# Layer 0 of a compressed interaction network: pairs of fields packed into full tiles, and a remainder stacked three times in one

## The chip, the cores and the metric

One core of a Trainium2 chip runs the whole program in one launch. The metric is the device time in microseconds. Engines are named PE (TensorE, matmul), DVE (VectorE), ACT (ScalarE), POOL (GpSimd) and SP (SyncE, which only issues DMAs here). The core has 16 DMA engines.

## The reference

2048 samples have 39 fields each; every field is an embedding row of 16 numbers, gathered from its own table. Three layers follow, with x0 the gathered fields and xk the first half of the layer before:

```
z = einsum('bhd,bkd,hks->bsd', x0, xk, W) + b     # 128 outputs s
z = relu(z); xk = z[:, :64]; direct.append(z[:, 64:])   # the last layer keeps all
logit = sum over d of concatenate(direct)
h = concatenate(logit, dense_ctx); three dense layers 272 -> 512 -> 256 -> 1
```

In layer 0 xk is x0 itself, so the product of fields f and g appears twice, and the kernel adds the two weights: 39 x 40 / 2 = 780 pairs of fields.

## The kernel before, in words

The samples go in 64 chunks of 32 samples, which with the 16 numbers of a row are 512 columns. POOL gathers the rows of a chunk by ten indirect DMAs, SP stores them turned into a DRAM tensor `x0_rows` of 58 rows (fields, and the first ones again) by 32768 columns, and SP and ACT load them back spread over partitions: `xa` (the 39 fields, three times below each other, 117 rows) and `xb` (the same fields shifted by 0, 1, 2 and then by 3 more for each of 7 tiles) for layer 0, `xh` (each field on 64 partitions, 20 tiles) for layers 1 and 2. A load of rows is 2 KB per row.

A layer is a sum over tiles: DVE multiplies a tile of `xb` or `xh` by the shared operand (`xa_ps`, a copy of `xa` in PSUM, or `x`, the relu output), and PE multiplies the product by the tile's weights into `z`. Three kinds of group share the cost of precision. WHOLE: the product and weights stay fp32, and a tile takes two instructions on PE. BY_DVE and BY_POOL: ACT rounds the product to fp32r (`high`, L877), DVE (L564) or POOL (L537) forms the remainder (`low`), and PE makes three fp32r passes: high by w_high, high by w_low, low by w_high. A half tile of layers 1 and 2 holds 64 products twice, so that its lower half can take the remainder (`half_passes`, two passes).

`GROUPS` lists, by stage (layer), the groups as (kind, first tile, number of tiles); all engines walk this list in its order, written out by hand. A step of the chunk loop is layer 1 of chunk c, layer 0 of chunk c + 1, layer 2 of chunk c. `load_pairs` (L415) on SP loads `xa` and `xb` once the products of layer 0 of the chunk before are made and the rows are stored; it stands between the stores and the load of `xh`, and before the store of features, which waits for sums that DVE makes right after layer 0. ACT's `copy_xa` (L863) is queued after the fifth rounding of layer 1 and waits for all pair loads; DVE's `layer0` (L623) waits for them and for the copy. SP, ACT and DVE each do their queue in order.

Before, layer 0 has 7 tiles: six of 3 shifts (117 rows) and one of 2 shifts (78 rows), in the groups WHOLE (tile 6), BY_DVE (0, 1), BY_POOL (2, 3), WHOLE (4, 5).

Of the kernel before, what the change touches and what calls it, by code (L numbers as in the profile page):

```python
# [28 lines left out]
CN = CB * D  # L29
# [9 lines left out]
T0 = -(-SHIFTS // JT)  # L39
LAST0 = (SHIFTS - JT * (T0 - 1)) * F  # L40
# [10 lines left out]
    0: [(WHOLE, 6, 1), (BY_DVE, 0, 2), (BY_POOL, 2, 2), (WHOLE, 4, 2)],  # L51
# [12 lines left out]
LAST_OUT_AFTER, XA_AFTER, FIRST_OUT_AFTER = 5, 4, 5  # L64
T1, T2 = 512, 256
# [6 lines left out]
STAGED = {0: 0, 1: T0, 2: T0 + TK}  # L72
TURNED = T0 + 2 * TK
ALL_TILES = TURNED + T0
# [20 lines left out]
class Group:  # L95


    def __init__(self, stage, chunk, g, counts, users):
# [7 lines left out]
        self.rows = 128 if stage else (LAST0 if first == T0 - 1 else JT * F)  # L106
# [19 lines left out]
def in_order_of_use(groups):  # L126

    behind = None
    for g in groups:
        late = g.split and not g.half  # L130
        if behind and (late or g.half or g.ends_layer):
# [56 lines left out]
def tower(nc, table, ids, row_base, ctx_t, staged, wt1, wt1c, wt2, cols, out):  # L188
# [6 lines left out]
    with ExitStack() as stack:  # L195
# [27 lines left out]
        xa = sb("xa", [JT * F, CN])  # L223
        xb = sb("xb", [JT * F, T0, CN])
# [34 lines left out]
        def split_places(weights, products):  # L259
# [8 lines left out]
                    "ctx": [w[0:CTX, CTX_AT:CTX_AT + MB], w[0:CTX, CTX_AT + MB:CTX_AT + 2 * MB]],  # L268
# [9 lines left out]
        assert ctx_end + MB // S <= len(SPLIT_TILE)  # L278
# [30 lines left out]
        x0_loaded = sem("x0_loaded")  # L309
        xa_copied = sem("xa_copied")  # L310
# [72 lines left out]
        N_GROUPS = len(firsts)  # L383
        W_READY = sum(g.split + g.half for g in firsts)
# [11 lines left out]
        def _(sp):  # L396
# [35 lines left out]
            def chunk(c):  # L432
# [7 lines left out]
                if not c.known or c.n >= 1:  # L440

                    wait_made(sp, 0, c - 1)
                load_pairs(c)
# [3 lines left out]
                elif c.n == 1:  # L447

                    sp.wait_ge(w_ready, W_READY)
                    sp.wait_ge(w_rounded, N_GROUPS)  # L450
# [15 lines left out]
            for i, (at, n) in enumerate([(0, T0), (TURNED, T0), (T0, TK), (T0 + TK, TK)]):  # L466
# [89 lines left out]
        def _(dve):  # L556
            def low_parts(g, c):
# [4 lines left out]
                part = slice(H, 128) if g.half else slice(0, g.rows)  # L562
                into = (high if g.half else low)[part, g.split_slot, 0:n, :]
# [5 lines left out]
            def products(stage, c, spread, shared, second=None):  # L569
# [3 lines left out]
                for g in groups(stage, c):  # L573
# [17 lines left out]
                    t = slice(g.tiles[0], g.tiles[0] + n)  # L591
                    dve.tensor_tensor(  # L592
# [452 lines left out]
```

## Time and profile before

| | |
|---|---|
| median of 3 runs | 2424.73 us (2424.66 to 2425.77) |
| profiled execution, its own time | 2426.18 us |
| its span, first to last instruction | 2424.2 us |
| PE busy | 2343.5 us, 97% |
| DVE busy | 2253.4 us, 93% |
| POOL busy | 2004.7 us, 83% |
| ACT busy | 1306.0 us, 54% |
| DMA queue q1 (SP) | 304354 packets, 310.69 MB, 52.9% of 16 engines |
| DMA queue q10 (ACT) | 78864 packets, 159.39 MB, 21.5% |
| mean granted clock of TensorE | 0.994 |

Busy time is the time in which an engine had an instruction under way. The share of the DMA is over the 16 DMA engines together; where transfers of one engine overlap it can read a little over 1. Matmuls are pipelined, so the pace of PE is the distance of their starts, not their length.

### The profile page before, as it was taken

Reading aid. Unit: us, or ns where it says so; the run is one execution under the profiler, and the core shown is the slowest. Engines: PE = TensorE matmul, PEld = TensorE weight load, DVE = VectorE, ACT = ScalarE, POOL = GpSimd, SP = SyncE. Lnnn points to the kernel's source line nnn. Section 1 sums busy time; section 2 is a strip of 40 time slices with the busy share of each in tenths; the row PEclk is TensorE's granted clock in tenths of the full one; section 3 lists DMA queues with packets and bytes.
Section 4 is the critical chain, followed back from the end, with each engine's and each line's share of the span. In section 5 each row is a group of like instructions: output and inputs, shape, how many; then the busy total and the mean of one; then the engine's idle time right before and its main releaser. Section 6 shows DMA issues by size and latency. Waiting matters only on the chain.

```text
span 2424.2 us, 32379 instructions
## 1 busy us (share of the span) xinstructions
PE 2343.5 (97%) x7936; PEld 1497.1 (62%) x7936; DVE 2253.4 (93%) x2241; ACT 1306.0 (54%) x1534; POOL 2004.7 (83%) x1284
## 2 busy tenths in 40 slices
PE   1699999999999999999999999999999999999999
PEld 0466666666666666666666666666666666666655
DVE  2699999999999999999999999999999999999973
ACT  2355555555555555555555555555555555555542
POOL 3689888988888898888889888888988888898630
PEclk9899999999999999999999999999999999999999
DMA  7878778877877887787788778778877877887710
GB/s 180 175 197 231 188 200 219 216 183 210 233 191 196 219 212 185 212 234 187 200 219 214 184 211 232 187 200 221 208 190 209 233 182 205 221 209 188 204 56 1
DMA packets 403715, 475.43 MB, mean 196 GB/s; under 512 B 171409, under 2 KB 180625, under 8 KB 403425
## 3 DMA queue, kind: packets, MB, share of 16 engines
q1 hardware_dynamic: 304354, 310.69, 52.9%
q10 hardware_dynamic: 78864, 159.39, 21.5%
q0 software_dynamic: 20480, 5.15, 1.8%
q8 instruction: 8, 0.13, 0.0%
q14 instruction: 9, 0.07, 0.0%
HBM read 465.41 MB, written 9.71 MB: 196 GB/s over the span
## 4 chain that ended last, share of the span: by engine, by line
PE 94%; POOL 2%; DMA 2%; issue 1%; SPq 0%; ACT 0%; DVE 0%; ACTq 0%; POOLq 0%
PE z L709 91%; POOL rows L507 1%; DMA xb<-x_rows 1%; POOL low L537 1%; DMA x_rows<-rows 1%; DMA rows<-table,index 0%; SPq L411 0%; PE x L804 0%; PE z L823 0%; PE prod_dve L804 0%; PE z L825 0%; PE z L782 0%; PE z L828 0%; PE x L805 0%; PE x L806 0%
## 5 line engine op out<-in xcount | busy, mean ns | idle before, releaser
L537 POOL TENSOR_TENSOR low<-prod_pool,high 128x1024 fp32r<-128x1024 f32 (+1 forms) x576 | 1379.9, 2396 | 220.8 <-ACT high L877 214.1
L709 PE MATMUL z<-prod_whole,w_whole 128*128 128x512 f32 (+2 forms) x2432 | 1129.4, 593 | 41.7 <-DVE prod_whole L592 41.7
L709 PE MATMUL z<-high,w_high 128*128 128x512 f32 (+1 forms) x1792 | 863.9, 482 | 31.2 <-ACT high L877 16.2
L877 ACT ACTIVATE high<-prod_pool 128x1024 fp32r<-128x1024 f32 (+1 forms) x576 | 610.9, 1061 | 405.8 <-DVE prod_pool L592 236.3
L709 PEld LDWEIGHTS z<-prod_whole,w_whole 128*128 128x128 f32 (+2 forms) x2432 | 460.9, 190 | 426.1 <-issue 364.1
L507 POOL DMA_INDIRECT rows<-table,index x640 | 613.5, 959 | 115.2 <-issue 99.7
L709 PE MATMUL z<-high,w_low 128*128 128x512 f32 (+1 forms) x1792 | 708.3, 395 | 0.0
L592 DVE TENSOR_TENSOR prod_pool<-xh,x 128x1024 f32<-128x1024 f32 x512 | 622.6, 1216 | 38.8 <-ACT x L855 33.6
L592 DVE TENSOR_TENSOR prod_whole<-xh,x 128x1024 f32<-128x1024 f32 (+1 forms) x576 | 615.7, 1096 | 7.6 <-PE z L709 1.6
L877 ACT ACTIVATE high<-prod_dve 128x1024 fp32r<-128x1024 f32 (+2 forms) x384 | 339.0, 883 | 497.0 <-DVE prod_dve L592 323.4
L709 PE MATMUL z<-low,w_high 128*128 128x512 f32 (+1 forms) x1664 | 553.5, 426 | 4.2 <-POOL low L537 4.2
L709 PEld LDWEIGHTS z<-high,w_high 128*128 128x128 f32 (+1 forms) x1792 | 339.5, 189 | 189.0 <-issue 112.2
L709 PEld LDWEIGHTS z<-high,w_low 128*128 128x128 f32 (+1 forms) x1792 | 339.9, 190 | 153.1 <-issue 91.2
L709 PEld LDWEIGHTS z<-low,w_high 128*128 128x128 f32 (+1 forms) x1664 | 313.8, 189 | 128.5 <-issue 60.3
L592 DVE TENSOR_TENSOR prod_dve<-xh,x 128x1024 f32<-128x1024 f32 (+1 forms) x320 | 323.8, 1012 | 15.3 <-DMA xh<-x_rows 10.9
L564 DVE TENSOR_TENSOR low<-prod_dve,high 128x1024 fp32r<-128x1024 f32 (+1 forms) x256 | 313.3, 1224 | 17.4 <-ACT high L877 13.1
L855 ACT ACTIVATE x<-z,cols_sb 64x512 f32<-64x512 f32 x256 | 166.6, 651 | 106.8 <-PE z L709 101.9
L592 DVE TENSOR_TENSOR prod_whole<-xb,xa_ps 78x512 f32<-78x512 f32 (+1 forms) x128 | 120.7, 943 | 23.4 <-ACT xa_ps L868 23.4
L564 DVE TENSOR_TENSOR high<-prod_dve,high 64x512 fp32r<-64x512 f32 x128 | 89.0, 695 | 9.8 <-ACT high L877 5.9
L860 ACT ACTIVATE direct<-z,cols_sb 64x512 f32<-64x512 f32 x128 | 87.7, 685 | 3.3
L592 DVE TENSOR_TENSOR prod_dve<-xb,xa_ps 117x1024 f32<-117x1024 f32 x64 | 78.0, 1219 | 0.0
L592 DVE TENSOR_TENSOR prod_pool<-xb,xa_ps 117x1024 f32<-117x1024 f32 x64 | 77.4, 1209 | 0.0
(59 smaller groups left out, 404.6 us busy)
## 6 DMA issues: line engine op xcount, KB each, us to landing
xh<-x_rows SPq DMA_DIRECT2D x63, 2560.0 KB, 17.8
xh<-x_rows ACTq DMA_DIRECT2D x63, 2432.0 KB, 19.2
xb<-x_rows SPq DMA_DIRECT2D x128, 546.0 KB
xb<-x_rows SPq DMA_DIRECT2D x64, 468.0 KB
xa<-x_rows SPq DMA_DIRECT2D x192, 78.0 KB
rows<-table,index POOLq DMA_INDIRECT x640, 5.4
xh<-x_rows SPq DMA_DIRECT2D x65, 128.0 KB, 20.5
x_rows<-rows SPq DMA_DIRECT2D x256, 20.0 KB, 1.6
```

Source lines behind the costliest of these rows:

```text
L507: pool.indirect_dma_start(rows_sb[p][0:n, j * D:(j + 1) * D], None, table, bass.IndirectOffsetOnAxis(ap=index[p][0:n, j:j + 1], axis=0),). ...
L537: pool.tensor_tensor(low[0:g.rows, g.split_slot, 0:n, :], prod_pool[0:g.rows, g.slot, 0:n, :], high[0:g.rows, g.split_slot, 0:n, :].bitcas ...
L564: dve.tensor_tensor(into, prod_dve_v[part, 0:n, :], high[part, g.split_slot, 0:n, :].bitcast(f32), ALU.subtract,).then_inc(low_by_dve, 1)
L592: dve.tensor_tensor(into[0:g.rows, 0:n, :], spread[0:g.rows, t, :], shared[0:g.rows, :].unsqueeze(1).broadcast_to([g.rows, n, CN]), ALU.mu ...
L709: return pe.matmul(z[stage][:, :], weights[0:g.rows, table[stage, g.tiles[i]], :], src[0:g.rows, i, :], start=g.begins_layer and first, st ...
L855: act.activation(xk[stage][half, :], z[stage][feed, :], ACT.Relu, bias=bias[stage][feed, :]).then_inc(relu_done[stage], 1)
L860: act.activation(direct[c.p][leave, :], z[stage][leave, :], ACT.Relu, bias=bias[stage][leave, :]).then_inc(relu_done[stage], 1)
L877: act.activation(high[0:g.rows, g.split_slot, 0:n, :], src[0:g.rows, 0:n, :], ACT.Copy).then_inc(high_ready, 1)
```

## The change

Layer 0 gets six tiles of 128 rows: the three shifts of 39 fields, and below them 11 more pairs (fields 0 to 10 with a field that lies 18 + tile further), loaded by two more DMAs of 11 rows. The last shift of the old tile 6 is gone; of its pairs, and of those not placed, 34 are left. They stand in a seventh tile, out of 40 rows that are loaded; pairs already placed have zero weights. The 40 rows stand at partitions 0 to 39 (their product is `high`, weighted by w_high), 64 to 103 (there DVE overwrites `high` with the remainder `low`, weighted by w_high), and in two halves of 20 at 40 to 59 and 104 to 123, both weighted by w_low (DVE overwrites 64 to 103 only, so these keep `high`). One pass on PE takes all three products. `xa_rest` is the first operand of that tile; it and the tile of `xb` are cleared once at the start by DVE. The 40 rows in their three places are loaded by 12 DMAs of 20 rows, each with the source pattern of 2 runs of 10 rows. The groups are now WHOLE (0, 1), BY_DVE (6, the rest), BY_POOL (2, 3), WHOLE (4, 5). The weights of the rest come from two staged tiles (one with the rows for w_high, one for w_low), joined by two DVE operations at the start.

```diff
-T0 = -(-SHIFTS // JT)
-LAST0 = (SHIFTS - JT * (T0 - 1)) * F
+T0 = SHIFTS // JT + 1
+REST = T0 - 1
+MORE = 128 - JT * F
+MORE_AT = JT * REST
+LEFT, LEFT_AT, LEFT_RUN, LEFT_STEP = 40, 10, 10, 19
+REST_LOW = 64
+FOR_HIGH_W = [(0, LEFT, 0), (0, LEFT, REST_LOW)]
+FOR_LOW_W = [(0, LEFT // 2, LEFT), (LEFT // 2, LEFT, REST_LOW + LEFT)]
...
-    0: [(WHOLE, 6, 1), (BY_DVE, 0, 2), (BY_POOL, 2, 2), (WHOLE, 4, 2)],
+    0: [(WHOLE, 0, 2), (BY_DVE, REST, 1), (BY_POOL, 2, 2), (WHOLE, 4, 2)],
...
+X0_LOADS = 2 * JT + 2 + 12
...
-        xa = sb("xa", [JT * F, CN])
-        xb = sb("xb", [JT * F, T0, CN])
+        xa = sb("xa", [128, CN])
+        xa_rest = sb("xa_rest", [128, CN])
+        xb = sb("xb", [128, T0, CN])
...
-                    "ctx": [w[0:CTX, CTX_AT:CTX_AT + MB], w[0:CTX, CTX_AT + MB:CTX_AT + 2 * MB]],
+                    "ctx": [w[0:CTX, CTX_AT:CTX_AT + MB], x[0:CTX, 4 + n1, :]],
...
             def load_pairs(c):
                 of = rows_of(c)
+                step = of.ap[0][0]
                 for jj in range(JT):
-                    n = (SHIFTS - jj + JT - 1) // JT
                     at = slice(jj * F, (jj + 1) * F)
                     sp.dma_start(xa[at, :], of[0:F, :]).then_inc(x0_loaded, 16)
-                    step = of.ap[0][0]
                     shifted = bass.AP(tensor=of.tensor, offset=of.offset + jj * step,
-                                      ap=[[step, F], [JT * step, n], [1, CN]])
-                    sp.dma_start(xb[at, 0:n, :], shifted).then_inc(x0_loaded, 16)
+                                      ap=[[step, F], [JT * step, REST], [1, CN]])
+                    sp.dma_start(xb[at, 0:REST, :], shifted).then_inc(x0_loaded, 16)
+                sp.dma_start(xa[JT * F:128, :], of[0:MORE, :]).then_inc(x0_loaded, 16)
+                shifted = bass.AP(tensor=of.tensor, offset=of.offset + MORE_AT * step,
+                                  ap=[[step, MORE], [step, REST], [1, CN]])
+                sp.dma_start(xb[JT * F:128, 0:REST, :], shifted).then_inc(x0_loaded, 16)
+                for first, end, to in FOR_HIGH_W + FOR_LOW_W:
+
+                    halves = range(2 * first // LEFT, 2 * end // LEFT)
+                    for s in halves:
+                        at = slice(to + (s - halves[0]) * LEFT // 2, to + (s - halves[0] + 1) * LEFT // 2)
+                        for rows, field in ((xa_rest, LEFT_AT + s), (xb[:, REST, :], LEFT_AT + LEFT_STEP)):
+                            runs = bass.AP(tensor=of.tensor, offset=of.offset + field * step,
+                                           ap=[[LEFT_STEP * step, 2], [step, LEFT_RUN], [1, CN]])
+                            sp.dma_start(rows[at, :], runs).then_inc(x0_loaded, 16)
...
-                part = slice(H, 128) if g.half else slice(0, g.rows)
-                into = (high if g.half else low)[part, g.split_slot, 0:n, :]
+                part = slice(H, 128) if g.half else slice(REST_LOW, REST_LOW + LEFT) if g.rest else slice(0, g.rows)
+                into = (high if g.stacked else low)[part, g.split_slot, 0:n, :]
...
+            dve.memset(xa_rest[:, :], 0.0).then_inc(rest_cleared, 1)
+            dve.memset(xb[:, REST, :], 0.0).then_inc(rest_cleared, 1)
...
+                def rest_pass(g):
+
+                    wait_count(pe, low_by_dve, c, g, g.of_kind + 1, BY_DVE)
+                    mm(g, w_high, SPLIT_TILE, high[:, g.split_slot, :, :], 0, True, True
+                       ).then_inc(products_used, 1)
...
-                act.wait_ge(x0_loaded, (c.n + 1) * 2 * JT * 16)
+                act.wait_ge(x0_loaded, (c.n + 1) * X0_LOADS * 16)
                 if not (c.known and c.n == 0):
                     wait_made(act, 0, c - 1)
-                act.activation(xa_ps[0:JT * F, :], xa[:, :], ACT.Copy).then_inc(xa_copied, 1)
+                act.activation(xa_ps[:, :], xa[:, :], ACT.Copy).then_inc(xa_copied, 1)
```

## Rows read from the trace of the kernel before

**Rows 1.** The page, part 1: busy us, share of the span, instructions.

```profile
PE 2343.5 (97%) x7936; PEld 1497.1 (62%) x7936; DVE 2253.4 (93%) x2241; ACT 1306.0 (54%) x1534; POOL 2004.7 (83%) x1284
```

**Rows 2.** Waits, whole span: engine, line, releaser, sum, times, longest.

```profile
PE z L709 <- DVE prod_whole L592: 41.7, 1, 41.7
ACT xa_ps L868 <- DMA xb<-x_rows: 37.0, 2, 22.9
DVE prod_pool L592 <- ACT x L855: 33.6, 64, 5.6
DVE prod_whole L592 <- ACT xa_ps L868: 23.4, 1, 23.4
```

**Rows 3.** Timeline of PE in layer 0: start, us, instruction, count.

```profile
1233.90 0.39 PE L709 MATMUL z<-high,w_low 117*128 117x512 f32 x1
...
1235.30 0.39 PE L709 MATMUL z<-high,w_low 117*128 117x512 f32 x1
...
1236.46 1.88 PE L709 MATMUL z<-prod_whole,w_whole 117*128 117x512 f32 x4
...
1238.40 0.40 PE L709 MATMUL z<-high,w_low 128*128 128x512 f32 x1
```

**Rows 4.** Timelines of DVE and ACT around layer 0 of one chunk.

```profile
1227.54 0.68 DVE L592 TENSOR_TENSOR prod_whole<-xb,xa_ps 78x512 f32<-78x512 f32 x1
1228.14 1.22 DVE L592 TENSOR_TENSOR prod_dve<-xb,xa_ps 117x1024 f32<-117x1024 f32 x1
...
1231.67 1.21 DVE L592 TENSOR_TENSOR prod_whole<-xb,xa_ps 117x1024 f32<-117x1024 f32 x1
1232.80 0.68 DVE L602 TENSOR_REDUCE chunk_feats<-direct 128x32 f32<-128x512 f32 x1
...
1222.85 0.60 ACT L868 ACTIVATE xa_ps<-xa 117x512 f32<-117x512 f32 x1
1224.22 1.02 ACT L877 ACTIVATE high<-prod_dve 128x1024 fp32r<-128x1024 f32 x1 [0.77 <-DVE prod_dve L592]
```

**Rows 5.** Timeline of SP's issues, one chunk; last, page: KB, us to landing.

```profile
1204.03 0.35 SPq L420 DMA_DIRECT2D xa<-x_rows  x1
...
1206.38 0.32 SPq L424 DMA_DIRECT2D xb<-x_rows  x1
1212.70 1.55 SPq L375 DMA_DIRECT2D xh<-x_rows  x2
...
1235.53 2.88 SPq L411 DMA_DIRECT2D x_rows<-rows  x6
...
1239.82 0.35 SPq L420 DMA_DIRECT2D xa<-x_rows  x1
...
x_rows<-rows SPq DMA_DIRECT2D x256, 20.0 KB, 1.6
```

**Rows 6.** Windows: stretch, engines' busy us; last PEclk, DMA share, GB/s.

```profile
1206.00:1214.00 8.00, 8.00 (x32) 5.71 (x31) 7.90 (x9) 5.44 (x7) 7.66 (x5) 1.00 0.87 189
1221.00:1228.00 7.00, 7.00 (x26) 4.70 (x25) 6.92 (x7) 4.88 (x6) 6.64 (x5) 1.00 1.05 400
...
40.50:43.50 3.00, 1.81 (x2) 0.50 (x2) 2.64 (x3) 1.04 (x2) 0.00 (x0) 1.00 1.07 209
```

**Rows 7.** DMA queue q1 in 1206-1214, then in 1221-1228: packets, MB, share.

```profile
q1 hardware_dynamic: 783, 1.50, 84.7%
...
q1 hardware_dynamic: 681, 1.39, 51.7%
```

**Rows 8.** Copies of xa on ACT, start and 57 later; DVE behind the second.

```profile
40.15 0.60 ACT L868 ACTIVATE xa_ps<-xa 117x512 f32<-117x512 f32 x1 [22.89 <-DMA xb<-x_rows]
86.88 0.60 ACT L868 ACTIVATE xa_ps<-xa 117x512 f32<-117x512 f32 x1 [14.13 <-DMA xb<-x_rows]
L868 ACT ACTIVATE xa_ps<-xa x57: 602/602/603, 303.1 to 2284.0; 117x512 f32<-117x512 f32 x57
...
94.78 1.21 DVE L592 TENSOR_TENSOR prod_whole<-xb,xa_ps 117x1024 f32<-117x1024 f32 x1
```

More of the change, by code:

```diff
@@ L105, in __init__ @@
         self.half = stage > 0 and first == HALF_TILE
-        self.rows = 128 if stage else (LAST0 if first == T0 - 1 else JT * F)
+        self.rest = stage == 0 and first == REST
+        self.rows = 128
+        self.stacked = self.half or self.rest
         self.split = self.kind != WHOLE
@@ L129, in in_order_of_use @@
     for g in groups:
-        late = g.split and not g.half
-        if behind and (late or g.half or g.ends_layer):
+        late = g.split and not g.stacked
+        if behind and (late or g.stacked or g.ends_layer):
             yield behind
@@ L382, in tower @@
         firsts = [g for stage in range(3) for g in PLAN[stage, 0]]
-        N_GROUPS = len(firsts)
-        W_READY = sum(g.split + g.half for g in firsts)
+        N_ROUNDED = sum(1 + g.rest for g in firsts)
+        W_READY = sum(g.split + g.half + g.rest for g in firsts)
         def weight_tiles(g):
@@ L743, in contract @@
                 for g in groups(stage, c):
-                    late = g.split and not g.half
+                    late = g.split and not g.stacked
                     if late:
                         high_passes(g)
-                    if behind and (late or g.half or g.ends_layer):
+                    if behind and (late or g.stacked or g.ends_layer):
                         low_passes(behind)
@@ L763, in chunk @@
                 contract(2, c)
-            pe.wait_ge(w_ready, sum(g.split for g in PLAN[0, 0]))
-            pe.wait_ge(w_rounded, len(GROUPS[0]))
+            pe.wait_ge(w_ready, sum(g.split + g.rest for g in PLAN[0, 0]))
+            pe.wait_ge(w_rounded, sum(1 + g.rest for g in PLAN[0, 0]))
             contract(0, Chunk(0, 0))
             pe.wait_ge(w_ready, W_READY)
-            pe.wait_ge(w_rounded, N_GROUPS)
+            pe.wait_ge(w_rounded, N_ROUNDED)
             over_chunks(pe, chunk)
@@ L931, in _ @@
                                ACT.Copy).then_inc(w_rounded, 1)
+                if g.rest:
+                    act.activation(w_low[:, to, :], stage_sb[:, T0:T0 + 1, :],
+                                   ACT.Copy).then_inc(w_rounded, 1)
             act.wait_ge(cols_loaded, 16)
@@ L988, with place @@
     w0 = a["L0_rec_w0"]
-    w0a = np.zeros((128, T0, S), w0.dtype)
-    w0b = np.zeros((128, T0, S), w0.dtype)
-    first = np.arange(F)
-    for j in range(SHIFTS):
-        second = (first + j) % F
-        at = slice(j % JT * F, (j % JT + 1) * F)
-        w0a[at, j // JT] = w0[first, second]
-        if j:
-            w0b[at, j // JT] = w0[second, first]
+    w0a = np.zeros((128, STAGED0, S), w0.dtype)
+    w0b = np.zeros((128, STAGED0, S), w0.dtype)
+    placed = set()
+    def place(f, g, at, tile):
+        if f != g:
+            w0b[at, tile] = w0[g, f]
+        w0a[at, tile] = w0[f, g]
+        placed.add(frozenset((f, g)))
+    for tile in range(REST):
+        for jj in range(JT):
+            for f in range(F):
+                place(f, (f + JT * tile + jj) % F, jj * F + f, tile)
+    for tile in range(REST):
+        for f in range(MORE):
+            second = (f + MORE_AT + tile) % F
+            if frozenset((f, second)) not in placed:
+                place(f, second, JT * F + f, tile)
+    left = []
+    for r in range(LEFT):
+        s, run, k = np.unravel_index(r, (2, 2, LEFT_RUN))
+        f = int(LEFT_AT + s + LEFT_STEP * run + k)
+        pair = (f % F, int(LEFT_AT + LEFT_STEP * (run + 1) + k) % F)
+        if frozenset(pair) not in placed:
+            placed.add(frozenset(pair))
+            left.append((r, pair))
+    for tile, copies in ((REST, FOR_HIGH_W), (T0, FOR_LOW_W)):
+        for r, pair in left:
+            for begin, end, at in copies:
+                if begin <= r < end:
+                    place(*pair, at + r - begin, tile)
+    assert len(placed) == F * (F + 1) // 2
     def by_fields(w):
```

40 lines of the change are left out of this document (28 added, 12 removed).

## The prediction

> **What bounds the kernel now.** I read five views, in this order. The page's busy shares show PE at 97% and DVE at 93% [rows 1]. The waits show that PE waited for another engine only in single events of the start; the one wait that comes back in every chunk is DVE's for ACT's `x`, 33.6 us in 64 times, so DVE has about 0.5 us to spare per chunk [rows 2]. The copies of `xa` into PSUM, one per chunk, give the period: 57 of them from 303.1 to 2284.0, so (2284.0 - 303.1)/56 = 35.37 us [rows 8]. PE fills it: 38 whole passes and 82 fp32r passes per chunk (2432/64 and (1792+1792+1664)/64). Then the SP queue and the windows of the DMA, because most lines of the diff are DMAs.
>
> **PE, part by part.** Back-to-back fp32r passes start 0.233 us apart ((1235.30 - 1233.90)/6); four whole passes take 1238.40 - 0.233 - 1236.46 = 1.71 us, 0.428 each [rows 3]. The 117 rows and 128 rows cost the same there. Layer 0 had 3 whole tiles (6 passes) and 4 split tiles (12 passes): 6 x 0.428 + 12 x 0.233 = 5.36 us. It gets 4 whole tiles (8 passes), 2 split tiles (6) and the one pass of the rest: 8 x 0.428 + 7 x 0.233 = 5.06 us. PE gains 0.305 us per chunk; over the 62 chunks behind the start, 18.9 us.
>
> **DVE, ACT, POOL.** DVE's layer 0 ran from 1227.54 to 1232.80, 5.26 us [rows 4]. Back to back, instructions of 1024 columns begin 1.13 us apart and one of 512 takes 0.60. A product of 1024 becomes one of 512 and the other way round, which cancels; a low part of 1024 becomes one of 512, at about 0.7 (estimate, between the two). Sum: -0.4 us, more than PE gains, so DVE stays behind PE. ACT rounds 512 columns in place of 1024 (-0.4 us). POOL's low part grows from 117 to 128 rows, by nothing I can see at 2.4 us. The new wait is PE's for the rest's low part, now second in the layer. DVE makes it before its last product of the layer, begun at 1231.67 so far [rows 4]; PE reaches it after the first whole group, at about 1232.8 + 1.7 = 1234.5: 3 us to spare. Behind it stand the four high passes of the pool group, no sooner than before. Two memsets, an eighth staged tile, three more weight operations: all before DVE's first product at 40.86, while it waits 23.4 us [rows 2]; nothing. At the end one more group must leave before the inputs of the MLP are rounded: six passes, 1.4 us at most, once; I take nothing, since PE still has passes of the last layer to run meanwhile.
>
> **SP and the DMAs of a chunk.** Before, six DMAs from 1204.03 to 1206.7; two `xh` loads follow at 1212.70, the other half is issued by ACT [rows 5]. After, 20: three `xa` and three `xb` of 39 rows, one of 11 rows each, and twelve of 20 rows. At 0.45 us each, the last is issued at about 1213. That moves SP's `xh` load by 0.5 us; the buffer is needed only after the next layer 2, and SP is idle from there nearly to its stores at 1235.53: nothing. Rows of 2 KB: 117 + 780 = 897 before, 128 + 768 + 240 = 1136 after.
>
> What decides is on how many of the 16 DMA engines they run. From 1206 to 1214 only the 39-row DMAs are in flight, with a backlog, and the share is 0.87; with DMAs of 64 rows it is 1.07 on one queue and 1.05 on two [rows 6]. So 0.847/1.073 x 16 = 12.6 engines: 39 = 13 x 3 is cut into 13 equal parts, 64 into 16. No equal cut, no use of the others. Each engine then moves 1.50 MB/2048/8 us/13, one row in 0.142 us; with 16 engines on one queue one in 0.157 (209 GB/s); with both queues full each queue still one in 0.165 (1.39 MB in 7 us) [rows 6, 7]. A queue's pace on an engine is thus nearly its own, about 0.16 us a row, whatever the other queue does.
>
> The twelve new DMAs read 20 rows as 2 runs of 10 (the source pattern's outermost count is 2). The trace has no DMA of that form; it is bounded by 2 engines (the cut falls on the outermost count, as every case in the trace can be read: 39, 64) and 10 engines (on the 20 partitions of the destination). I take 2: to cut at 10 the source would have to be cut inside its second dimension, and `xb`, whose second dimension of 7 would have allowed other cuts, ran on 13. Then engines 0 and 1 carry 12 x 10 = 120 rows more, in the same queue, behind their 70 of the other eight DMAs (9 + 54 + 7).
>
> The Trainium skill, in "DMA: Bandwidth & Descriptors", section "Why a DMA increments its semaphore by 16 and not by 1", says how a DMA from SP or ACT is spread: over the largest number up to 16 that divides the slowest dimension of both patterns, on the lowest-numbered engines. The share of 0.87 agrees for 39 rows; by that rule the new ones get 2 engines, by the other reading 10. No run here shows that form yet.
>
> **The sum by the likeliest.** Landing: first packets about 1.2 us after the issue at 1204.0 (an estimate; a whole small store lands in 1.6 [rows 5]); 70 rows x 0.142 = 9.9; 120 x 0.16 = 19.2; 0.5 for the last to count: 30.8 us, at 1234.8. ACT needs all of them for the copy of `xa` that it began at 1222.85, with 0.77 us free before its next rounding [rows 4]. It stands 12 us late, and with it every rounding queued behind on ACT, then DVE, POOL and PE. The loads can't start earlier, since they hang on the end of the same chain: copy of `xa`, to the end of DVE's layer 0, 8.7 us (86.88 to 94.78 + 1.21, less the 0.4 above; PE was no part of that stretch's chain) [rows 8]; from there to the next pair loads on SP 7.0 us (sums, features, six stores and their landing, 1232.80 to 1239.82) [rows 4, 5]. Period: 8.7 + 7.0 + 30.8 = 46.5 us in place of 35.37. As a check, one engine's queue: 70 + 120 rows and its 84 of SP's `xh` loads are 9.9 + 19.2 + 13.4 us, plus stores: 45 us. PE's gain is then gone in idle time.
>
> Start: the first copy came at 40.15 and moves by 120 x 0.157 = 18.8; the second, at 86.88, by twice that (its stores queue behind the longer first loads, its own loads are longer): 124.5. Then 62 x 46.5 = 2883, and what follows the last copy, 2424.2 - 2284.0 = 140.2 [rows 8]. Span 3148 us. The profiled execution took 2426.18 with a span of 2424.2; the median of the runs, 2424.73, is 0.5 over that span. Forecast: 3148 us, 30% slower.
>
> Bounds of the row's price on engines 0 and 1: 0.082 us (one engine's pace over both queues, 400 GB/s): landing after 21.4, period 37.1, time 2547. And 0.205 (the 69 rows per engine of the first chunk, between about 26 us and the copy at 40.15): landing after 36.2, period 51.9, time 3495.
>
> **The rivals.**
> A, faster: the 20-row DMAs are cut into 10. Ten engines get 24 rows more, 3.8 us; the loads are in at about 1219.5, before 1222.85, and the period is PE's. 2424.7 - 18.9, plus the start, where the loads are on the chain (23 and 14 us of ACT's waits for them are two events [rows 2]): about 2 x 4 us. 2414 us. For it: nothing in the trace excludes it. Against: the reading of the source pattern. It turns when more than some 50 rows of the new ones fall on one engine: then the landing passes 1224.
> B, as slow as the forecast for another reason: each small DMA is only begun when the one before has landed. A store of 20 KB lands in 1.6 us [rows 5]; 12 x 1.6 = 19.2 us, so about 3150 as well. Against: six such stores are issued in 2.9 us and all in 1.4 us later. The share in the new stretch would be near nothing, not two engines full.
> C, near no change: PE's gain is eaten by the start alone, because its DMAs cost some 9 us each of the two times (0.16 us x 55 rows on the fullest engine), while the period stays under. 2424.7 - 18.9 + 18 = 2424. It needs a cut between A and the forecast, such as 4 or 5 engines (48 to 60 rows), and stands on the edge of A's turning point.
>
> **Chances.** Forecast with its bounds 0.81, A 0.13, B 0.03, C 0.03. What a measurement can tell from no change is 0.2%, about 5 us. Faster 0.13, same 0.02, slower 0.85. Range: the forecast's cost terms move together; 2620 to 3480 leaves out A, C and the outermost of the bounds, some 0.2.
>
> **What would show it.** Right: ACT's copy of `xa` waits for the DMA `xb` or `xa_rest` in all chunks, 10 us or so each, 600 to 750 us in sum; the interval of its copies is 42 to 52 us; DMA share between the `xh` loads and the stores falls to about 2/16 for several us; PE's busy share falls near 75% and PE waits for ACT or DVE in every chunk; SP's wait for DVE's sums before the features shrinks only by what its own added issues take. PE's layer 0, taken alone, is 15 passes with the row spacing above. Wrong: the copies 35.1 us apart and ACT's waits for the DMA at two events; then the cut was finer, and A holds. If the copies wait but by 2 us, the price of a row was the low one.

## The result, and the profile after

The changed kernel takes 3947.41 us (median of 4 runs, 3941.78 to 3950.44) where the kernel before takes 2424.69 (2423.95 to 2425.77): the ratio is 1.628, 95% interval 1.6252 to 1.6303. The forecast was 3148 us with a range of 2620 to 3480. The direction was right, and so was the place of the loss. The size was missed by 800 us, and the range did not hold it.

The page of the changed kernel: its span, part 1 (busy us, share, instructions), the line of q1 from part 3, and the first line of part 4 (the chain that ended last, by engine).

```profile
span 3945.8 us, 33856 instructions
...
PE 2466.0 (62%) x7744; PEld 1550.7 (39%) x7744; DVE 2247.8 (57%) x2244; ACT 1272.9 (32%) x1535; POOL 2017.6 (51%) x1284
...
q1 hardware_dynamic: 322594, 342.16, 44.1%
...
DMA 42%; SPq 28%; DVE 11%; issue 9%; PE 6%; ACT 2%; POOL 1%; DVEq 1%; ACTq 0%; POOLq 0%
```

PE has 192 passes fewer than before [rows 1], three for each of 64 chunks, as planned. Yet its busy share fell from 97% to 62%, and the chain now runs through DMAs and through SP, which issues them. Its busy time is 2466.0 us for fewer passes where it was 2343.5: after each idle stretch, in which the granted clock stands at 0.50 (the 1.2 GHz level, first window below), PE begins slow: the second window, in which it works again, has 0.73 in the mean.

Waits of the changed kernel, whole span (sum, times, longest):

```profile
POOL low L571 <- ACT high L934: 1724.0, 208, 26.2
ACT xa_ps L925 <- DMA xb<-x_rows: 1638.8, 64, 34.7
DVE low L599 <- ACT high L934: 1547.7, 63, 29.9
...
PE z L758 <- ACT high L934: 1403.6, 64, 27.9
```

Read the second row first. ACT's copy of `xa` waited for the DMA in two events before [rows 2]; now it waits in all 64, 25.6 us each. The other three rows are its followers: ACT's roundings stand behind the copy in ACT's order, and POOL, DVE and PE wait for those roundings.

The copies themselves (grouped row: count, ns, first and last start), against [rows 8], and two neighbours from the timeline:

```profile
L925 ACT ACTIVATE xa_ps<-xa x63: 601/601/601, 115.6 to 3806.9; 128x512 f32<-128x512 f32 x63
```

```profile
2021.04 0.60 ACT L925 ACTIVATE xa_ps<-xa 128x512 f32<-128x512 f32 x1 [25.15 <-DMA xb<-x_rows]
...
2080.30 0.60 ACT L925 ACTIVATE xa_ps<-xa 128x512 f32<-128x512 f32 x1 [25.39 <-DMA xb<-x_rows]
```

The period is (3806.9 - 115.6)/62 = 59.54 us in place of 35.37. SP's issues in between, against [rows 5]:

```profile
2037.27 0.35 SPq L440 DMA_DIRECT2D xa<-x_rows  x1
...
2047.15 0.63 SPq L456 DMA_DIRECT2D xa_rest<-x_rows  x1
2047.88 3.32 SPq L456 DMA_DIRECT2D xb<-x_rows  x1
2051.30 2.56 SPq L456 DMA_DIRECT2D xa_rest<-x_rows  x1
2053.97 4.85 SPq L456 DMA_DIRECT2D xb<-x_rows  x1
2058.99 18.64 SPq L395 DMA_DIRECT2D xh<-x_rows  x2
```

From the copy at 2021.04 to the next pair loads at 2037.27 is 16.2 us; from there to the copy at 2080.30 it is 43.0. The last small DMAs and the `xh` loads take SP several us each: the queue is full and SP stands in it. Windows of the changed kernel (columns as in [rows 6]), and q1 in the second one (packets, MB, share of 16 engines):

```profile
2006.00:2014.00 8.00, 0.00 (x0) 0.00 (x0) 0.00 (x0) 0.00 (x0) 0.00 (x0) 0.50 1.05 202
2022.00:2031.00 9.00, 8.37 (x23) 5.61 (x23) 8.32 (x9) 4.92 (x7) 5.20 (x3) 0.73 0.14 27
```

```profile
q1 hardware_dynamic: 113, 0.23, 13.3%
```

In the second window almost nothing but q1 moves, and it uses 13.3% of 16 engines: 2.1 engines, full. Each moves 113/2 packets in 9 us, a row in 0.159 us. These are not the small rows: the copy at 2021.04 waited for all of those, and the next pair loads are issued at 2037.27. They are rows of SP's `xh` load, which engines 0 and 1 still have to do because the small rows stood before them. So the window shows two engines that are behind the others, and the price of an `xh` row alone; experiment 5 shows that of a small row alone. Now q1 and q10 (ACT's queue) from 2054 to 2061, while the small rows and ACT's `xh` load are under way:

```profile
q10 hardware_dynamic: 653, 1.34, 97.8%
q1 hardware_dynamic: 48, 0.09, 6.3%
```

The small rows on their two engines: 48 packets in 7 us, 0.29 us each and somewhat more for a row, since a few of the 48 are completion marks. The forecast had 0.16. Here is the term that was mis-sized.

### The profile page after: what moved, and what is told of

Same layout as the page of the kernel before. It is cut to its first block, busy times and chain, and to the rows that moved or that the text cites. A ratio compares the mean times of both kernels' runs of the same rounds, so it can differ in the third digit from the quotient of the medians.

```text
span 3945.8 us, 33856 instructions
## 1 busy us (share of the span) xinstructions
PE 2466.0 (62%) x7744; PEld 1550.7 (39%) x7744; DVE 2247.8 (57%) x2244; ACT 1272.9 (32%) x1535; POOL 2017.6 (51%) x1284
## 3 DMA queue, kind: packets, MB, share of 16 engines
q1 hardware_dynamic: 322594, 342.16, 44.1%
## 4 chain that ended last, share of the span: by engine, by line
DMA 42%; SPq 28%; DVE 11%; issue 9%; PE 6%; ACT 2%; POOL 1%; DVEq 1%; ACTq 0%; POOLq 0%
DMA xb<-x_rows 40%; SPq L456 21%; DVE prod_whole L628 6%; PE z L758 4%; SPq L431 2%; SPq L443 2%; SPq L440 2%; ACT high L934 2%; DVE prod_pool L628 2%; DVE prod_dve L628 2%; DMA x_rows<-rows 1%; DVE chunk_feats L638 1%; DVE high L599 1%; SPq L444 1%; SPq L447 1%
## 5 line engine op out<-in xcount | busy, mean ns | idle before, releaser
L571 POOL TENSOR_TENSOR low<-prod_pool,high 128x1024 fp32r<-128x1024 f32 x576 | 1378.4, 2393 | 1729.8 <-ACT high L934 1724.0
L758 PE MATMUL z<-high,w_high 128*128 128x512 f32 x1728 | 889.8, 521 | 1419.5 <-ACT high L934 1403.6
L758 PE MATMUL z<-prod_whole,w_whole 128*128 128x512 f32 x2560 | 1185.4, 593 | 53.7 <-DVE prod_whole L628 53.7
L599 DVE TENSOR_TENSOR low<-prod_dve,high 128x1024 fp32r<-128x1024 f32 x192 | 234.9, 1224 | 1549.2 <-ACT high L934 1547.7
L758 PEld LDWEIGHTS z<-high,w_high 128*128 128x128 f32 x1728 | 359.2, 208 | 1618.6 <-ACT high L934 1437.8
L934 ACT ACTIVATE high<-prod_pool 128x1024 fp32r<-128x1024 f32 x576 | 610.3, 1060 | 442.0 <-DVE prod_pool L628 413.1
L758 PE MATMUL z<-high,w_low 128*128 128x512 f32 x1664 | 707.1, 425 | 0.0
L758 PEld LDWEIGHTS z<-prod_whole,w_whole 128*128 128x128 f32 x2560 | 486.5, 190 | 469.2 <-issue 419.0
L758 PE MATMUL z<-low,w_high 128*128 128x512 f32 x1536 | 563.4, 458 | 2.9 <-POOL low L571 2.9
L758 PEld LDWEIGHTS z<-high,w_low 128*128 128x128 f32 x1664 | 347.4, 209 | 141.5 <-issue 76.1
L758 PEld LDWEIGHTS z<-low,w_high 128*128 128x128 f32 x1536 | 321.9, 210 | 135.4 <-issue 56.1
L912 ACT ACTIVATE x<-z,cols_sb 64x512 f32<-64x512 f32 x256 | 166.6, 651 | 53.6 <-PE z L758 46.2
```

What stands on the lines that cost most here:

```text
L571: pool.tensor_tensor(low[0:g.rows, g.split_slot, 0:n, :], prod_pool[0:g.rows, g.slot, 0:n, :], high[0:g.rows, g.split_slot, 0:n, :].bitcas ...
L599: dve.tensor_tensor(into, prod_dve_v[part, 0:n, :], high[part, g.split_slot, 0:n, :].bitcast(f32), ALU.subtract,).then_inc(low_by_dve, 1)
L758: return pe.matmul(z[stage][:, :], weights[0:g.rows, table[stage, g.tiles[i]], :], src[0:g.rows, i, :], start=g.begins_layer and first, st ...
L912: act.activation(xk[stage][half, :], z[stage][feed, :], ACT.Relu, bias=bias[stage][feed, :]).then_inc(relu_done[stage], 1)
L934: act.activation(high[0:g.rows, g.split_slot, 0:n, :], src[0:g.rows, 0:n, :], ACT.Copy).then_inc(high_ready, 1)
```

## The experiments

Each kernel ran beside the kernel before on one chip. Experiments 5, 6 and 8 to 12 rest on one execution each, the others on four to six. "Period" is the distance of ACT's copies of `xa`, from the grouped row as above; "landing" is the time from SP's first pair load to ACT's copy, in one chunk unless it is called a mean over the chunks (the two differ by at most 0.8 us where both were taken).

**1. The cut: runs of ten.** Both operands of the rest stand in one tensor; each small DMA reads one run of ten rows for both. Still 12 DMAs and 240 rows, but the outermost count is 10.

```
-  ap=[[LEFT_STEP * step, 2], [step, LEFT_RUN], [1, CN]]
+  ap=[[step, LEFT_RUN], [(LEFT_STEP - s) * step, 2], [1, CN]]
```

> The changed kernel, but each of the 12 small DMAs reads one run of 10 rows for both operands of the rest (outermost count 10) in place of two runs of 10 for one operand (outermost count 2). Same rows, same 240 x 2 KB, same number of DMAs. Theory (all small rows lie on two DMA engines): now ten engines get 24 rows each, the pair loads land before ACT wants them, the copies of xa come 35.1 us apart, time 2414 us (2407 to 2421). Rival 1 (each small DMA costs a fixed time of its own): as many DMAs as before, so the copies stay 59 us apart and the time at about 3950. Rival 2 (the DMA engines are short of bandwidth with 6% more bytes): also still above 3000.

Measured: 2801.45 us, ratio 1.155 (1.1534 to 1.1566), period (2646.1 - 138.1)/61 = 41.1, landing 23.2. Three quarters of the loss, 1146 of 1523 us, was the two engines. The number of engines can also be counted. Below, the page's rows of q1 for the kernel of experiment 2 (no small DMAs), this one, and that of experiment 6 (the same rows in three DMAs):

```profile
q1 hardware_dynamic: 305698, 310.69, 54.3%
```

```profile
q1 hardware_dynamic: 328738, 342.18, 60.2%
```

```profile
q1 hardware_dynamic: 322978, 342.16, 61.8%
```

Per chunk this one has (328738 - 305698)/64 = 360 packets more than without small DMAs, the changed kernel (322594 - 305698)/64 = 264, and the three-DMA kernel 270. With 240 rows taken off, 120, 24 and 30 completion packets are left for 12, 12 and 3 DMAs: 10, 2 and 10 engines for one DMA. But the forecast's rival A gave such a cut 2414 us, and it came to 2801. Two things were missing.

**2. No loads of the rest at all.** The twelve DMAs are gone and the rest's tile holds zeros, so its 34 pairs are left out; all engines do the same work.

```
-  X0_LOADS = 2 * JT + 2 + 12
+  X0_LOADS = 2 * JT + 2
-  for first, end, to in FOR_HIGH_W + FOR_LOW_W:
-      ...
```

> The changed kernel without the 12 small DMAs; the rest tile stays zero, so its 34 pairs are left out of the sum, and all else runs. Theory: the rest of the change is what the passes on PE say, 62 x 0.305 us less than before, 2406 us (2403 to 2410). Rival (the new wait of PE for the rest's low part, or the order of groups, costs something): above 2415.

Measured: 2446.55 us (2445.53 to 2448.66), ratio 1.0087 (1.0072 to 1.0103), period (2306.0 - 124.2)/61 = 35.77. Not faster, so 40 us against the expected 2406 are lost outside the DMAs. The groups of DVE by form (count, busy us and mean ns) and the timeline name the place:

```profile
L619 DVE TENSOR_TENSOR prod_dve<-xb,xa_rest 128x512 f32<-128x512 f32 x64 | 133.4, 2084 | 0.0
...
L619 DVE TENSOR_TENSOR prod_dve<-xh,x 128x512 f32<-128x512 f32 x128 | 88.2, 689 | 11.2 <-DMA xh<-x_rows 11.2
```

```profile
1203.79 2.41 POOL L562 TENSOR_TENSOR low<-prod_pool,high 128x1024 fp32r<-128x1024 f32 x1
1204.61 2.15 DVE L619 TENSOR_TENSOR prod_dve<-xb,xa_rest 128x512 f32<-128x512 f32 x1
```

Two products of 512 columns: with `x` from PSUM 689 ns, with `xa_rest` from SBUF 2084. The slow one ends at 1206.76, 0.56 us after POOL's operation ends at 1206.20: it looks as if it had stood still until POOL was done and then taken its own time.

**3. The same, with the second operand from PSUM.**

```
-  other = xa_rest if g.rest else shared
+  other = shared
```

> As in the run without the twelve small DMAs (34 of the 741 pairs are left out, the rest tile holds zeros), but the rest's product on DVE takes its second operand from PSUM (the copy of xa) in place of SBUF. That run took 2446.6 us; its rest product took 2.08 us a time in place of about 0.69, ending when POOL's own 2.4 us operation ended. Theory L (a DVE operation with both operands in SBUF waits for GpSimd's, and the reverse): the product falls to 0.6 to 0.8 us, DVE gets 1.4 us a chunk back, the period falls from 35.77 to about 35.1, and the time is 2446.6 - 62 x 0.65 = 2406 us (2400 to 2412). Rival M (the product is slow for another reason, or the time above before comes from the longer layer-0 order on PE): the time stays at 2440 to 2450.

Measured: 2405.57 us against 2426.05 for the kernel before beside it, ratio 0.9918 (0.9902 to 0.9935); period (2262.9 - 123.0)/61 = 35.08. The product's group:

```profile
L619 DVE TENSOR_TENSOR prod_dve<-xb,xa_ps 128x512 f32<-128x512 f32 x64 | 44.1, 689 | 0.0
```

(The expectation counts 741 pairs; layer 0 has 780.) That settles two terms. A product of two SBUF operands costs 1.4 us more beside POOL's operation here, 41 us in all (2446.6 - 2405.6). And the saved passes are worth 20.5 us, where the forecast had 18.9. The Trainium skill, "SBUF — State Buffer", section "SBUF: two separate sides", states this lock: a VectorE operation with two SBUF inputs and a GpSimd operation that reads SBUF hold a shared pair of ports in turn, each for its whole length. The runs agree, with 2084 and 689 ns. The cost goes with what is left of POOL's operation: in the changed kernel the product begun at 2026.01, 0.56 us before POOL's ended, took 1.11 us. Its mean there is 1098 ns, and in experiment 6 it is 1498.

**4. ACT's `xh` load later, with runs of ten.** ACT issues it only after its copy of `xa`.

```
-  if not final:
-      load_odd_fields(c + 1)
...
-  during1[XA_AFTER] = lambda: copy_xa(c + 1)
+  during1[XA_AFTER] = copy_and_load
```

> As the version whose twelve small DMAs read one run of ten rows each (2801 us, period 41.1, landing 23.2 us after the issue), but ACT issues its half of the next xh only after its copy of xa, so no ACT queue moves loads while the pair loads are under way. Theory X (the two queues fight for the same engines while both move xh or small rows): the pair loads land 16 to 18 us after the issue, the period is 35.5 to 37, the time 2446 to 2530. Theory D (each small DMA has a fixed cost on its engines, whoever else is active): landing stays at 22 to 24 us, the period at 40 to 41.5, the time at 2750 to 2810. If xh itself becomes late, ACT's or DVE's first wait in layer 1 is for the DMA xh, and the time is no lower than 2700.

Measured: 3049.83 us, ratio 1.2575 (1.2554 to 1.2596), period 45.4, landing 1222.0 - 1203.2 = 18.8. The landing came down by 4.4 us, to just above the 16 to 18 of theory X, and the time went up: from the copy to the next pair loads it takes 25.9 us in the mean over the chunks, where it took 17.7. What was moved out of the way comes later, in the way of SP's stores and `xh` loads. X holds for the landing only.

**5. The changed kernel with ACT's `xh` load later.** The same edit on the changed kernel itself.

> The changed kernel, but ACT issues its half of the next xh only after its copy of xa. Theory Q (the small rows landed in 43.9 us and not in the predicted 30.8 because ACT's xh rows shared engines 0 and 1 with them): the small rows move at about 0.16 us each and the pair loads land 29 to 33 us after their issue; the time need not fall with it, since the two engines still have the same 350 rows per chunk and xh comes late: 3700 to 4200 us. Theory D (fixed cost per DMA): landing stays above 40 us.

Measured: 3635.17 us, below the range of theory Q, period (3494.6 - 106.0)/62 = 54.7. ACT's copies and the start of SP's pair loads between them:

```profile
1197.05 0.60 ACT L925 ACTIVATE xa_ps<-xa 128x512 f32<-128x512 f32 x1 [19.08 <-DMA xb<-x_rows]
...
1209.60 5.25 SPq L431 DMA_DIRECT2D x_rows<-rows  x6
...
1222.17 0.35 SPq L440 DMA_DIRECT2D xa<-x_rows  x1
...
1251.42 0.60 ACT L925 ACTIVATE xa_ps<-xa 128x512 f32<-128x512 f32 x1 [19.89 <-DMA xb<-x_rows]
```

The landing is 1251.42 - 1222.17 = 29.25 us where the changed kernel has 43.0, so the 12 us that the forecast's 30.8 missed are there only beside ACT's load. But 29.25 is near 30.8 partly by luck. In the trace's completions the first five small DMAs land about 0.8 us apart, the last seven 1.3 to 1.9. The first lie before SP's own `xh` load, issued behind them at 1236.21, has begun; q1 from 1235 to 1237:

```profile
q1 hardware_dynamic: 52, 0.10, 12.7%
```

Two engines are full again, and 48 of the 52 packets are rows: a small row alone takes 2 x 2/48 = 0.083 us. While the other 14 engines move SP's `xh` rows it takes about twice that, 0.17. In the changed kernel, with ACT's `xh` load beside it, ten rows of an engine take 3.0 to 3.4 us, twice as much again; its last small DMAs, when both `xh` loads are nearly through, land 0.8 to 1.0 us apart.

From the copy to the next pair loads it takes 25.1 us here in place of 16.2: the six stores, issued from 1209.60, are landed only shortly before 1222. ACT's late rows still move on the same two engines in that time, 22 to 27 packets per 2 us from 1212 to 1220 on q10. So the gain in the landing is in part lost again. Engines 0 and 1 have 70 + 120 + 84 + 76 = 350 rows per chunk (pair loads, small rows, SP's and ACT's `xh`). At 0.154 us (217 and 205 GB/s, where two queues share one pace in experiment 10, are 0.151 and 0.160) this is 54 us, an estimate, near the period here. It is no floor that a run has shown: the kernel before has 229 rows on these engines, 35.3 us by the same price and also near its period, though the DMA share was only 0.36 from 1200 to 1204.

**6. Three DMAs in place of twelve.** As experiment 1, but 40 partitions by 2 rows each; they hold other fields, so the rest's sums are not the reference's.

```
+  for to in (0, LEFT, 2 * LEFT):
+      both = bass.AP(..., ap=[[step, LEFT], [(XROWS - LEFT - 1) * step, 2], [1, CN]])
+      sp.dma_start(xb[to:to + LEFT, REST:REST + 2, :], both)
```

> As the version with runs of ten (2801 us), but the 240 small rows come in three DMAs of 40 partitions by 2 rows, not in twelve; they hold other fields, so the rest tile's sums are wrong numbers. Bytes and rows are the same; 10 engines carry 24 rows each as before. Theory D (fixed cost per DMA on its engines, 0.7 to 1.1 us each): nine DMAs fewer take 6 to 9 us from the landing, which falls from 23.2 to 14 to 17 us, the period to 35.5 to 36.5, and the time is 2440 to 2500. Theory R (cost per row, 24 rows at 0.3 us or more): landing 22 to 24 us, time 2760 to 2810.

Measured: 2466.55 us, period (2325.0 - 135.2)/61 = 35.90. Rows, bytes and engines are those of experiment 1, the time is 335 us less, in the range of theory D; the landing is 19.3 us in the mean over the chunks, where D said 14 to 17. So small DMAs seem to have a price of their own on the engines that they touch: nine fewer per chunk gave 41.1 - 35.9 = 5.2 us, 0.58 for each DMA that brings an engine only two rows, and at least that, since 35.9 is next to the floor of experiment 2. The edit also changed which partitions an engine writes, and experiment 9 shows that this can matter; the two weren't taken apart.

**7. Three DMAs and the operand from PSUM.** Both edits (the rest's sums are not the reference's either).

> Both repairs at once: the rest's 240 small rows come in three DMAs (other fields, so the rest tile's sums are wrong numbers) and the rest product takes its second operand from PSUM (the copy of xa). If the two costs are independent, the 40.9 us that the PSUM operand gave in the version without small DMAs come off the 2466.6 of the three-DMA version: 2426 us (2415 to 2432), so a layer 0 with one pass less earns nothing even when the loads are in three DMAs. Rival (the lock and the late loads hide each other): 2406 to 2415, or 2440 and more.

Measured: 2455.76 us (2448.05 to 2469.69), ratio 1.0114 (1.0097 to 1.0132), period (2329.0 - 138.3)/61 = 35.91. The forecast of 2426 missed, and its rival, 2440 or more, held: the two costs are not a sum. The profile is that of the slowest execution (2469.69 us), so the period goes with that time. Its landing is 1250.62 - 1230.45 = 20.2 us in one chunk, 19.6 in the mean, and with the 16.3 us from the copy to the next pair loads this is the period. The rest's product fell from 1498 ns to 690, and ACT's waits for the DMA rose from 136.6 us (experiment 6) to 188.1, both in 62 waits: the 0.8 us per chunk that DVE got back went into that wait. In this form too the rest's rows cost more than the passes that they save.

**8. Half of the rows, as many DMAs.** Two runs of five in each of the twelve two-run DMAs; half of the rest's rows are left out.

```
-  [step, LEFT_RUN]
+  [step, LEFT_RUN // 2]
```

> The changed kernel with its twelve two-run DMAs as they are in number and form, but two runs of five rows each in place of two of ten, so half of the rest's rows are left out. Engines 0 and 1 then carry 290 rows per chunk in place of 350. Theory R (the cost is per row on the two engines, 0.154 us where both queues are counted): 60 x 0.154 = 9.2 us less, a period of 50.3 in place of 59.5, and a time of 3947 - 62 x 9.2 = 3375 us (3250 to 3500). Theory D (a fixed cost for each DMA on an engine): period above 57, time above 3800.

Measured: 3237.28 us, period (3095.0 - 105.5)/62 = 48.2. 60 rows fewer on each of the two engines gave 11.3 us of the period, 0.19 a row, where theory R had 0.154; the time is 13 us below its range. Theory D, with a period above 57, is out. Of the two it is theory R.

**9. Where the small rows are written.** Experiment 1 with every twelfth partition in place of ten neighbours (the rest's rows stand in wrong places).

> The version with runs of ten (2801 us), with each small DMA's ten rows written to every twelfth partition in place of ten neighbours, so the rest tile's rows stand in wrong places. Rows, bytes, number of DMAs and engines are the same. Theory P (neighbouring partitions share a way into SBUF, which slows the small DMAs): landing falls from 23.2 us to 16 to 18, time 2450 to 2550. Theory D (fixed cost per DMA): landing 22 to 24 us, time 2760 to 2830.

Measured: 3014.51 us, period 44.9, landing 26.2 in the mean over the chunks. Neither theory: spreading the partitions made it worse by 3.8 us per chunk. Why isn't settled.

**10. Two queues and the halves of the partitions.** Three probes of the kernel before. In the first, SP and ACT each load both halves for a range of `xh` tiles, lower half first, so that both write the same half at the same time. In the second, ACT takes the upper half first. In the third, ACT's load of the upper half reads the even fields, so the odd fields are left out.

```
-  load_fields(act, c, 1, xh_loaded[c.p], 0, HALF_TILE)
+  load_fields(act, c, 0, xh_loaded[c.p], SECOND, TK)          # first probe
+  load_fields(act, c, 1, xh_loaded[c.p], SECOND, HALF_TILE)
+  load_fields(act, c, 1, xh_loaded[c.p], 0, HALF_TILE, 0)     # third probe
```

> The kernel before, but SP and ACT each load a range of tiles of xh for both halves of the partitions, the lower half first, so that both queues write partitions 0 to 63 (from even fields) at the same time and then 64 to 127. Theory P (two queues of an engine go side by side only when they write different halves, or read different fields): the DMA rate with both queues busy falls from 400 GB/s to about 210, xh lands some 10 us later, and the time hardly moves (2425 to 2440), since there were 17 us to spare. Rival Q (a queue's pace of 0.16 us per row is its own whatever it writes): the rate stays at 400.

> As h1_same_half, but ACT starts with the upper half of the partitions (odd fields) while SP starts with the lower one. Theory P: 400 GB/s with both queues busy, as before. Rival R (the finer DMAs of h1 slow the queues by themselves): about as h1.

> The kernel before, with one change: ACT's load of the upper half of the xh tiles reads the even fields, the same rows that SP's load of the lower half reads, so the odd fields are left out of the numbers. Theory H (two queues keep their pace as long as they write different halves of the partitions): both queues move 180 packets or more per 2 us each, 400 GB/s in all, and the time is 2425 us. Rival S (what matters is the rows of memory that are read): both fall to about 100 packets per 2 us each, and the time is near 2700, as with both queues on the same half.

Measured: 2702.06, 2430.1 and 2426.34 us. The first probe's rate came out as theory P said, its time didn't (2425 to 2440 forecast). Windows with both queues busy, first probe, then second (different halves, then the same), then third:

```profile
1213.00:1217.00 4.00, 4.00 (x13) 2.29 (x13) 3.95 (x6) 2.99 (x5) 3.29 (x3) 1.00 1.07 205
```

```profile
1220.00:1224.00 4.00, 4.00 (x14) 2.30 (x13) 3.96 (x4) 2.69 (x3) 3.67 (x3) 1.00 1.05 328
1224.00:1228.00 4.00, 4.00 (x16) 2.60 (x15) 3.97 (x5) 3.21 (x5) 3.66 (x4) 1.00 1.07 217
```

```profile
1221.00:1228.00 7.00, 7.00 (x27) 4.89 (x26) 6.92 (x8) 4.34 (x6) 6.64 (x5) 1.00 1.05 398
```

The DMA share reads 1.05 to 1.07 in all of them, at 205 GB/s and at 398: a full share says that the engines have work, not at what pace. In these windows two `xh` loads keep their pace beside each other when they write different halves, and share one pace when they write the same. [rows 6] showed the first case alone, and the forecast made a rule of it. Different halves aren't enough either: in experiment 5, from 1204 to 1210, engines 0 and 1 move 12 to 13 packets of SP's `xh` per 2 us beside ACT's load into the other half, 0.31 us a row. The Trainium skill, "SBUF — State Buffer", section "Door 1: The DMA port swizzle (why `[64,N]` ≈ `[32,N]`)", says that partitions 0 to 63 reach one half of the DMA ports and 64 to 127 the other; 205 and 398 GB/s agree. Its section "Can I just issue two DMAs to hit both halves?" says that two DMAs on the two halves gain only 6% over a single one; here two moved 398 GB/s and a single queue 209 [rows 6], and the measurement decides.

**11. Is it the half, for the small rows?** The changed kernel with only those six small DMAs that write partitions 0 to 63, then with only those that write 64 to 127; each leaves out half of the rest's rows.

```
+  if not (to < REST_LOW):       # second kernel: to >= REST_LOW
+      continue
```

> The changed kernel with only those six of its twelve two-run DMAs that write partitions 0 to 63; the other six are left out, and with them half of the rest's rows. Engines 0 and 1 carry 60 small rows each. ACT's xh load, which moves at the same time, writes partitions 64 to 127. Theory H (on one engine two queues keep 0.157 us a row each when they write different halves, and fall to 0.31 when they write the same): 11 us for the larger DMAs and 60 x 0.157 = 9.4: landing 20 to 24 us after the issue, period 36 to 40, time 2480 to 2700. Rival E (a short DMA pays 0.31 us a row beside another queue whatever half it writes): landing 29 to 33, as with twelve DMAs of half the rows, time 3050 to 3300.

> The changed kernel with only those six of its twelve two-run DMAs that write partitions 64 to 127, the half that ACT's xh load writes at the same time; half of the rest's rows are left out. Same rows, bytes, DMAs and engines as in the run with the six of the lower half. Theory H: 11 + 60 x 0.31 = 30 us, landing 28 to 33, period 45 to 49, time 3050 to 3300. Rival E (the half doesn't matter): within 2% of the run with the lower six.

Measured: 3114.79 and 3121.70 us, periods 46.2 and 46.3. The same; for the small rows the half does not decide, and rival E holds. Experiment 8 has as many small rows in twice as many DMAs, and a period of 48.2: 2 us per chunk for six DMAs.

**12. Or the source?** An `xh` load reads each row 64 times, a small DMA reads its rows once. The kernel before with ACT's half reading different rows (numbers of that half left out), and the changed kernel with one row ten times in each run (wrong rows in the rest).

```
-  ap=[[0, H], [2 * step, end - first], [1, CN]]
+  ap=[[step, H // 2], [step, HALF_TILE], [1, CN]]     # two DMAs of 32 partitions
-  [step, LEFT_RUN]
+  [0, LEFT_RUN]                                        # in the changed kernel
```

> The kernel before, with one change: ACT's load of the upper half of the xh tiles reads a different row for each partition (in two DMAs of 32 partitions), where it read one row 64 times over; the numbers of that half are left out. Bytes and destinations are the same. Theory S (two queues on an engine keep their pace of 0.157 us a row each only where the row that is read is the same one again, as in xh, and share 0.155 in sum where rows are read once): while both queues are busy they move about 100 packets per us in sum in place of 185, 205 to 230 GB/s, and the time is 2550 to 2750. Rival (where the rows are read from doesn't matter): 390 to 400 GB/s, 2425 to 2435.

> The changed kernel with its twelve two-run DMAs reading one row ten times in each run in place of ten rows, so the rest's operands are wrong rows. Number, size, destinations and engines are the same. Theory S: beside ACT's xh load the small rows keep 0.16 us a row; landing falls from 43.9 us to 29 to 34 after the issue, period 45 to 50, time 3050 to 3300. Rival: as the changed kernel, 3900 to 3960.

Measured: 2425.23 us with 394 GB/s in the window 1221 to 1228, and 3965.5 us. Both are the rival's case: reading distinct rows or the same one made no difference that counts. So it is shown that ACT's `xh` load about doubles the price of a small row on engines 0 and 1 (experiment 5). By which mechanism stays open, and also why SP's `xh` rows on the other engines already make it 0.17 where it is 0.083 alone. Not tried: SP's `xh` load held back until the small rows have landed.

## Why the prediction was right or wrong

Its own sum, term by term: second copy 124.5, then 62 x 46.5, then 140.2. Measured: 115.6, 62 x 59.54, 3945.8 - 3806.9 = 138.9. The start was 8.9 us too long and the end right. The period was 13.0 us too short, 808 us in all: less the 10 us of the two ends, that is the error of the span.

- **PE gains 0.305 us per chunk.** Right: experiment 3 has a period of 35.08 where 35.37 - 0.305 = 35.07 was due, and 20.5 us for the 18.9.
- **DVE loses nothing.** Wrong. The rest's 512-column product was priced at 0.60 us by a row with one operand in PSUM; the change puts both in SBUF. In the changed kernel it took 1.10 us, so 0.4 us per chunk over a product with one operand in PSUM, little beside the 13 of the landing; without the small DMAs it takes 2.08 and alone turns -20 us into +22 (experiments 2 and 3). No rival held it; A and C would have failed on it too.
- **ACT, POOL, the earlier low part, memsets, weights.** Nothing, as said: experiment 3 has them all and comes out where PE's term puts it.
- **SP issues 0.45 us apart.** The two-run DMAs take 0.63 each, 0.73 apart, and the last three 2.6 to 4.9, behind a full queue. It costs nothing by itself: SP waits for the engines there, not they for SP.
- **Two engines.** Right (2 completion packets per DMA; 12.7% of 16 engines while small rows alone move, experiment 5).
- **0.16 us a row, "whatever the other queue does".** The step that failed. A small row took 0.083 us with nothing beside it, about 0.17 while SP's own `xh` rows moved on the other engines, and 0.30 to 0.34 beside ACT's `xh` load, which is where most of them ran. The landing was 43.0 us for the predicted 30.8, and 29.25 when ACT's load was moved away. The premise came from one window in which two `xh` loads wrote different halves. The bounds had the same gap: 0.082 and 0.205 were both taken from rows without a small load beside an `xh` load.
- **8.7 + 7.0 us from the copy to the next pair loads.** Right: 16.2.
- **The check of one engine's queue, 45 us.** It left out ACT's 76 rows because the queues were held to be independent. With them, all 350 rows at 0.154 are 54 us, which would have warned that 46.5 needs independent queues. By the same failed step the landing was short: 70 rows at 0.142 and then 120 + 76 at 0.154, with the forecast's 1.2 and 0.5, are 41.8 us (an estimate) of the 43.0.
- **Rival A (2414 us).** Its cut was built in experiment 1: 2801 us. It lacked what twelve small DMAs cost over three (experiment 6) and the product (experiment 2). Its turning point was sound: it had the landing pass 1224, 20 us after the issue, and near there the period leaves the floor (experiment 7).

None of the kernels with the reference's work that ran beats the one before. Experiment 3 does (2405.6), without the rest's 34 pairs; with as many rows loaded in the best form that was tried it is 2455.8. A copy of the rest's own operand into PSUM was not tried.

## What to carry to other kernels

When a change adds DMAs, write down for each how many engines it gets (the outermost count of its pattern), then add up, for the fullest engine, the rows of all queues in one period, and price them at the pace of one queue unless a row shows that these very loads run beside each other. Such a sum is a warning and no floor. When an elementwise operand moves from PSUM to SBUF, price the instruction by a row with both operands in SBUF beside the other engine's work. And a hidden landing has a length from which it shows: here about 35.1 - 16.3 = 18.8 us (period of experiment 3, less the way from the copy to the next pair loads), and the three DMAs of experiment 7 stood at 19.6 in the mean.

## What the runs showed of the hardware

- A DMA of 20 rows with an outermost count of 2 ran on 2 engines, one with 10 on 10: 1146 us of this kernel's time for the same bytes.
- Each DMA leaves one completion packet per engine used, so the packets of a queue tell the cut without a timeline (24, 120 and 30 per chunk).
- Twelve DMAs of 2 rows per engine took 5.2 us per chunk more than three of 8 rows per engine, 0.58 for each of the nine; the partitions that an engine wrote differed too.
- A row of a small DMA took 0.083 us on its engine alone, about 0.17 with SP's `xh` load on the other engines, 0.30 to 0.34 beside ACT's `xh` load.
- Two queues moved 205 GB/s when both wrote one half of the partitions and 398 when they wrote different ones, at the same DMA share of 1.05 to 1.07.
- A DVE product of 512 columns with both operands in SBUF took 2084 ns beside POOL's 2.4 us operations in experiment 2 (1098 in the changed kernel), and 689 with one operand in PSUM.
- Writing ten rows to every twelfth partition in place of neighbours made the kernel 213 us slower; unexplained.
